# Two conditional matrix products with residuals on one Trainium2 core: idle transposes, own PSUM banks for one block, and stores from ScalarE

## The reference, cut to what matters

```
def cond(x, index, weights):                       # weights: (8, 64, 64) or (200, 64, 64)
    return einsum('bct,bcd->bdt', x, weights[index])

x = x + cond(x, itok_B_0_7, L0_cond_weights)       # 8 matrices
x = x + cond(x, itok_B_1_198, L1_cond_weights)     # 200 matrices
```

## Time and profile before

| | |
|---|---|
| median of 3 runs | 93.66 us (93.46, 93.66, 95.83) |
| the profiled execution's own time | 94.32 us |
| its span, first to last instruction | 92.5 us |
| busy: PE, DVE, ACT, POOL | 72.8, 60.9, 50.6, 23.8 us |
| moved by the DMA engines | 35.92 MB, 388 GB/s over the span |
| chain that ended last, by engine | PE 73%, DMA 13%, DVE 6%, ACT 1% |

### The profile page before, as it was taken

One profiled execution on the slowest core, in us unless ns is written; L12 is line 12 of the kernel. 1 busy time (PEld: TensorE's weight loads), 2 busy tenths in 40 slices (PEclk: granted clock), 3 DMA queues, 4 the chain that ended last, 5 costly groups with the idle time before them and its releaser, 6 DMA issues.

```text
span 92.5 us, 2284 instructions
## 1 busy us (share of the span) xinstructions
PE 72.8 (79%) x836; PEld 38.7 (42%) x836; DVE 60.9 (66%) x115; ACT 50.6 (55%) x95; POOL 23.8 (26%) x124
## 2 busy tenths in 40 slices
PE   0400009999299999999999999999999999999700
PEld 0200008899154545435445544754444444444200
DVE  0086003389527887888778788878788788787740
ACT  2300001468626776777567677677576676676630
POOL 4220009989999989000000000000000000000000
PEclk9999999999999999999999999999999999999995
DMA  0999999999999999999999999999999999879695
GB/s 16 330 457 390 430 395 420 413 411 405 416 405 404 400 411 404 409 407 416 398 411 413 418 409 418 420 409 420 420 421 418 414 418 416 361 310 388 276 402 228
DMA packets 9180, 35.92 MB, mean 388 GB/s; under 512 B 721, under 2 KB 850, under 8 KB 9042
## 3 DMA queue, kind: packets, MB, share of 16 engines
q1 hardware_dynamic: 8880, 33.56, 90.4%
q0 software_dynamic: 144, 2.10, 5.4%
q10 hardware_dynamic: 146, 0.13, 0.5%
HBM read 19.01 MB, written 16.78 MB: 387 GB/s over the span
## 4 chain that ended last, share of the span: by engine, by line
PE 73%; DMA 13%; DVE 6%; issue 2%; DVEq 1%; ACT 1%; POOLq 0%; ACTq 0%
PE psum L225 61%; DMA w_rows<-in_L_cond_weights_dram,cond 10%; PE psum L206 7%; PE psum L187 6%; DVE w L244 5%; DMA cond<-in_itok_B_dram 3%; DVEq L64 1%; DVE xy L266 1%; ACT m_diag L258 1%; DVE w_rows L306 0%; POOLq L160 0%; ACTq L250 0%; POOLq L151 0%
## 5 line engine op out<-in xcount | busy, mean ns | idle before, releaser
L225 PE MATMUL psum<-xy,m_diag 64*128 64x512 f32 x256 | 56.6, 594 | 0.0
L266 DVE COPY xy<-psum 64x512 f32<-64x512 f32 x64 | 43.7, 684 | 12.7 <-PE psum L225 11.7
L266 ACT COPY xy<-psum 64x512 f32<-64x512 f32 x64 | 37.2, 581 | 19.1 <-PE psum L225 18.3
L225 PEld LDWEIGHTS psum<-xy,m_diag 64*128 64x128 f32 x256 | 24.4, 187 | 27.7 <-issue 27.1
L168 POOL COPY w0b<-w0t 64x64 f32 x112 | 21.6, 235 | 10.3 <-DMA w_rows<-in_L_cond_weights_dram,cond 8.5
L187 PE MATMUL psum<-ident,w_rows 128*64 128x128 f32 x64 | 9.5, 323 | 9.3 <-DVE w_rows L306 9.3
L244 ACT COPY w<-psum 64x256 f32<-64x256 f32 x16 | 5.8, 364 | 15.3 <-PE psum L187 14.5
L187 PEld LDWEIGHTS psum<-ident,w_rows 128*64 128x64 f32 x64 | 8.4, 158 | 10.7 <-DVE w_rows L306 9.8
L244 DVE COPY w<-psum 64x256 f32<-64x256 f32 x16 | 6.7, 417 | 3.4 <-PE psum L187 3.0
L206 PE MATMUL psum<-w,w0b 64*32 64x64 f32 x512 | 6.5, 224 | 1.8 <-ACT m_diag L258 0.9
L258 DVE TENSOR_SCALAR m_diag<-psum,mask 128x256 f32<-128x256 f32 (+2 forms) x14 | 6.7, 517 | 1.9 <-PE psum L206 1.7
(11 more groups left out here) (6 smaller groups left out, 0.8 us busy)
## 6 DMA issues: line engine op xcount, KB each, us to landing
xy<-in_x_dram SPq DMA_DIRECT2D x15, 1024.0 KB, 19.5
out_dram<-xy SPq DMA_DIRECT2D x15, 1024.0 KB, 11.1
xy<-in_x_dram SPq DMA_DIRECT2D x2, 512.0 KB, 7.4
out_dram<-xy SPq DMA_DIRECT2D x2, 512.0 KB, 3.4
w_rows<-in_L_cond_weights_dram ACTq DMA_DIRECT2D x1, 128.0 KB, 2.6
cond<-in_itok_B_dram SPq DMA_DIRECT2D x1, 0.5 KB, 2.4
subjects<-in_itok_B_dram ACTq DMA_DIRECT2D x1, 0.5 KB
w_rows<-in_L_cond_weights_dram,cond POOLq DMA_INDIRECT x1, 9.5
```

What stands on the lines that cost most here:

```text
L225: last = nc.tensor.matmul(psum[:, 2 * (s % Y_RING) + h, :], m_diag[rows, odd, v % M_RING, j, :], xy[rows, s, j * T:(j + 1) * T], start=j = ...
L266: copy(xy[rows, s, i * T:(i + 1) * T], psum[HALVES[i], 2 * (s % Y_RING) + h, :]).then_inc(done, 1)
```

## The change

1. After the four transposes of W0, TensorE does 52 more transposes of the same rows (`WARM`), into banks 0 to 5, which nobody reads. They wait for nothing; the transposes of W1 stand behind them.
2. The products of block 1 go to banks 4 and 5 (`M_BANKS`), all others stay in 6 and 7. So `products(1)` no longer waits for the scalings of block 0; later blocks wait as before.
3. The stores leave SP. ScalarE issues the store of slots s - 2 and s - 1 right after its own copies of slot s (s even), and those of slots 30 and 31 singly at its end. SP keeps the loads and the final waits.
4. The mask is written by VectorE at its start, in eight memsets of 32 x 1, in place of five by GpSimd (one of 128 x 2 and four of 32 x 1).

```diff
+    M_BANKS = [6, 4, 6, 6, 6, 6, 6]
...
+    WARM = 52
...
             for v in range(2, UNITS):
                 load(2 * v, 2)
-            def store(s, n):
-
-                sp.wait_ge(s_y_v, 2 * (s + n))
-                sp.wait_ge(s_y_s, 2 * (s + n))
-                sp.dma_start(out_view[:, s:s + n, :], xy[:, s:s + n, :]).then_inc(s_out[s // 2], 16)
-
-            for v in range(UNITS - 1):
-                store(2 * v, 2)
-            store(SLOTS - 2, 1)
-            store(SLOTS - 1, 1)
             for v in range(UNITS):
                 sp.wait_ge(s_out[v], 32 if v == UNITS - 1 else 16)
...
-            nc.gpsimd.memset(mask[:, :], 0.0).then_inc(s_zeros, 1)
-            pool.wait_ge(s_zeros, 2)
-            for r, rows in enumerate(QUARTERS):
-                nc.gpsimd.memset(mask[rows, r % 2:r % 2 + 1], 1.0).then_inc(s_mask, 1)
-            pool.wait_ge(s_mask, SLOT)
...
             last.then_inc(s_w0_turned, 1)
+            for n in range(WARM):
+                nc.tensor.transpose(psum[0:C, n % W1_RING, 0:P], w0_rows[:, n % ROWS, :], ident[:, :])
...
-                if k >= 1:
+                if k >= 2:
+
                     pe.wait_ge(s_m_v, 2 * k)
                     pe.wait_ge(s_m_s, 2 * k)
...
-                                last = nc.tensor.matmul(psum[QUARTERS[r], M_BANK + odd, at:at + C],
+                                last = nc.tensor.matmul(psum[QUARTERS[r], M_BANKS[k] + odd, at:at + C],
...
+        def store(s, n):
+
+            nc.scalar.wait_ge(s_y_v, 2 * (s + n))
+            nc.scalar.wait_ge(s_y_s, 2 * (s + n))
+            nc.scalar.dma_start(out_view[:, s:s + n, :], xy[:, s:s + n, :]).then_inc(s_out[s // 2], 16)
+
...
-            eng.wait_ge(s_mask, SLOT)
+            eng.wait_ge(s_mask, 2 * SLOT)
...
                 for s in range(2 * first, 2 * (first + n)):
                     copy_y(eng, copy, y_done, odd, s)
+                    if odd and s % 2 == 0 and s > 0:
+
+                        store(s - 2, 2)
...
         @block.vector
         def _(dve):
+            for r, rows in enumerate(QUARTERS):
+                for b in range(2):
+                    nc.vector.memset(mask[rows, b:b + 1], 1.0 if b == r % 2 else 0.0).then_inc(s_mask, 1)
+
...
             copies(act, nc.scalar.copy, nc.scalar.mul, s_w1_s, s_m_s, s_y_s, 1)
+            store(SLOTS - 2, 1)
+            store(SLOTS - 1, 1)
```

More of the change, by code:

```diff
@@ L47, in bass_cond_residual_kernel @@
     M_RING = 8
-    M_BANK = 6
+    M_BANKS = [6, 4, 6, 6, 6, 6, 6]
     Y_RING = 3
@@ L258, in copy_m @@
                 scale(to[:, b, :, :, :],
-                      psum[:, M_BANK + odd, at:at + n * J * C].rearrange("q (w e i) -> q w i e", i=J, e=Q),
+                      psum[:, M_BANKS[k] + odd, at:at + n * J * C].rearrange("q (w e i) -> q w i e", i=J, e=Q),
                       mask[:, b:b + 1]).then_inc(done, 1)
```

## The result

The changed kernel takes 98.35 us (median of 4, 97.71 to 101.61) against 93.8 us: ratio 1.0475, 95% interval 1.0395 to 1.0555. That is about 4.5 us slower where 1.3 us faster was forecast, and outside the range. The kernel before took between 93.4 and 99.3 us in the executions that were timed beside the experiments, so the ratios here compare only the executions near each kernel's fastest.

The account below looks back on a forecast made before the run. TensorE's unbroken stream was taken as the bound, with DMA engines able to give back about 1.8 us. Lead of 2.3 plus 0.45 (2.8), less 1.5 for later stores, gave 1.3: from 93.66 to 92.4 us, range 91.5 to 94.2.

Parts of the forecast that it names:

- D: Load and store queues share their depth, so ScalarE's first store is accepted only at 37.94 us; 96.3 us; chance 0.07.
- Unread transposes, the idle time: Before W1 lands: 1.9 us idle keeps TensorE's clock high, so W1 is turned 2.3 us earlier.
- Rival B: TensorE's clock is low again when W1 comes; lead only 0.45 to 1.1 us; 94.7 us, at best 94.1; chance 0.10.
- Unread transposes, the instructions: After W0's transposes: the 52 were priced by TensorE's time alone, 17 at 206 ns and 35 at 112 ns.
- Own banks: Start of the stream: block 1's products run while block 0's M is scaled; 0.45 us of lead.
- Mask, priced at 0: Kernel start: VectorE's eight memsets fit while it has nothing to do, and GpSimd wins nothing; 0 us.
- Stores on ScalarE: Kernel end: the store of slots 28 and 29 waits for ScalarE's copy of slot 30; costs 1.5 us.
- C: ScalarE's first store waits while SP is inside a load's issue; TensorE loses 1.6 us; 94.0 us; chance 0.13.
- The limit of 1.8 us: Late in the run: however early TensorE is, the DMA engines can give back only about 1.8 us at unchanged rate.

Follow-up runs that it names:

- e2: The kernel before with only the 52 unread 128 x 128 transposes added; ratio 1.0146.
- e10: The changed kernel with its two blocks of four units split into four of two; ratio 1.0112.
- e13: The changed kernel with the mask written by GpSimd as before; ratio 1.0198.
- e14: The kernel before with 68 unread transposes, own banks, blocks of two units and the stores on ScalarE one slot behind; ratio 0.9881.
- e11: The kernel before with own banks, blocks of two units and 68 unread 128 x 128 transposes; 93.14 us, ratio 0.9916.
- e1: The changed kernel without its 52 unread transposes; 95.2 us, ratio 1.0104.
- e3: The changed kernel with 76 more unread transposes, of 32 x 32, behind the 52; ratio 0.9889.
- e4: The kernel before with 52 unread transposes of 32 x 32; 99.88 us, no ratio.
- e9: e4 without all stores but those of the last two slots; one execution, no time given, no gap in the products.
- e5: The kernel before with own banks for block 1's M and nothing else; ratio 0.9988.
- e7: The kernel before with the mask written by VectorE and nothing else; ratio 1.0339.
- e6: The kernel before with the stores issued by ScalarE one slot behind and nothing else; ratio 1.0042.
- e8: The kernel before with own banks for block 1 and 128 unread transposes of 64 x 64; ratio 1.0376.

## Why the prediction was wrong, by its own steps

The sum had 2.3 for the turning of W1 and 0.45 for the banks, less 1.5 for the late stores: 1.3 us won. The trace has 0.6 and 0.5, less 0.4 for the stores, 0.8 for W1's later landing and 3.2 for the gaps: 3.3 us lost. No rival reached the measured time either: the slowest, D, stood at 96.3 us, by a mechanism that did not occur.

**Unread transposes, the idle time.** The step took 1.9 us of idle time, "nearer to the short one", and so the high level. It failed: with W1 seen at 14.3 it was 2.6 us, the clock fell and was low until 18.5, and the lead of 2.3 us was 0.6. Rival B had this mechanism. With 2.6, 2.8, 3.3 and 5.0 us of idle time (the changed kernel, e2, e10, e13) the clock fell before the turning of W1 or at its start, with 0.75 (e14) it stayed; whether 1.9 would have kept it, no run shows. The rest of the step holds where no idle time is left (e11): W1 in 7.15 us and the stream at 23.45.

**Unread transposes, the instructions.** The step priced 52 transposes as TensorE's time alone. That they also move everything behind them in the instruction stream was no term of the sum and no rival, and it was the largest: 3.2 us. e1, e2, e3 and e4 show it by the count, e9, in one execution, that full DMA engines are the other half of it, e10 that shorter runs of products avoid it. The trace of before has no gap that could have warned of it; it does list the instruction queue's transfers.

**Own banks.** 0.45 us forecast, 0.5 in the trace of e5; its effect on the time is too small to be measured.

**Mask, priced at 0.** The step looked only at who was idle. In the changed kernel's trace W1 was seen 0.8 us later, and all six profiled kernels with VectorE's mask have W1 at 14.1 us or later. What that costs is not settled: the ratios are 1.034 alone (e7, against the quicker half of the kernel before's executions), about 2.6% inside the change (e13), and with e1 at 1.0% in all hardly anything. The cause of the later landing is open.

**Stores on ScalarE.** Priced at 1.5 us; measured 0.4 to 0.5 (e1's end, the issue 1.63 us against 1.99 ahead of the last matmul's end, and e6's ratio, whose interval holds nothing as well), and none in e14. The mis-sized term is the wait: the store was taken to follow ScalarE's copies of the next slot, but it was issued at 32.30, when the first of them (32.23) had just begun. It waits only for what its semaphores name, the slots before. Rivals C and D fall with the same row, an issue of 0.41 us beside SP's blocked one.

**The limit of 1.8 us** held: no version got more by its ratio (1.2% in e14, 1.1 us), and e11's trace has 1.2 us of span.

## What to carry to other kernels

An added instruction can cost more than its time: it moves everything behind it in the instruction stream, and if a piece then ends inside a dense run of small instructions while the DMA engines are full, the engine stands for a microsecond or more with no releaser in the profile. Where a chain says "issue" in the middle of such a run, change the count or shorten the run before looking for a cause elsewhere. Work that is to keep the clock high must reach close up to the work that it is for (0.75 us short of it was enough here, 2.6 was not), and the small transposes tried here didn't do it.

## What the runs showed of the hardware

- Instruction pieces: 16 KB, about 1 us each, and with full DMA engines some 2.8 us later against the program than with idle ones (e9 against e4). TensorE went on 1.30 to 1.47 us after the end of the piece in each of eight gaps.
- TensorE's clock: raised by back-to-back 128 x 128 transposes, not by 14 us of 64 x 64 (e8), not held by 2.4 us of 32 x 32 (e3). It fell with idle times of 2.6 and 2.8 us (changed kernel, e2), not with 0.75 (e14), and after 2.5 us in which TensorE was busy for 0.66 (e7). Before its first record in a trace the clock column reads 1.00, at 206 ns a transpose too.
- A DMA issue on ScalarE did not wait for the copies ahead of it in the same program to end (issued at 32.30, the copy running from 32.23), and took 0.35 to 0.42 us, while SP stood in an issue too (0.41).
- Loads and stores mixed in two queues moved 414 GB/s, against 409 and 418 for mostly loads and for stores.
